# Two chunks of 96 rows, or 128 and 64: the first product of a feed-forward block on TensorE's two halves

## The chip, the core and the metric

The kernel runs on one core of a Trainium2 chip. The metric is the device time of one execution in microseconds (us), and the median of some runs is given. TensorE multiplies matrices (PE in the profile; PEld is its loading of weights), VectorE is DVE, ScalarE is ACT, GpSimd is POOL, and SyncE (SP) issues transfers. The engines run their own streams of instructions and wait for each other by semaphores.

## The reference

A tower of two layers over 16 sequences of 128 tokens with 192 features, all in fp32: token embedding, an attention with running sums, a feed-forward block with a routed attention of its own, a second attention, and a mixture of 8 experts. The change touches the last lines of the feed-forward block:

```python
h = hidden_states + merged
n2 = _ln(h, g2, b2)                       # over 192 features
ffn = jax.nn.gelu(n2 @ W1 + bf1, approximate=False) @ W2 + bf2    # W1: 192 x 768, W2: 768 x 192
return h + ffn
```

## The kernel before

Four sequences make a group (G = 4, 512 tokens), and there are four groups. The stages are written out by hand, one list of calls for each engine. `front` works on group 0 alone. `joint(ta, tb)` runs three times: it lays the first half of the network for group `ta` between the second half for group `tb`, which begins with the feed-forward product. `back` does the second half of the last group alone, with its tokens in two halves of 256 (`hf`), and starts the experts.

The feed-forward product in a joint stage runs so. `n4_T` transposes the normalized tokens `xb` on TensorE into PSUM, two chunks of 96 features for each sequence (C = 2, CW = 96). `n4T_evac` on ScalarE brings them to SBUF in `xT` and applies scale and bias (`g2c`, `b2c`). `ffn_up(tb, j)`, for each of six slices of 128 hidden features (FJ = 6), multiplies 128 x 128 weights `w_up` with all 512 tokens and adds two such products, one for each chunk: the chunks have 96 rows, and rows 96 to 127 of the weights are zero. `ffn_gelu(tb, j)` on ScalarE takes the slice through gelu to `hid` (in the buffer `big`), and `ffn_down(tb, b)` multiplies it by `w_down` once all six gelus are done. The slices lie in the PSUM pairs `PD`, `PC`, `PD`, so slices 4 and 5 wait for gelus 0 and 1.

Between the slices stand two small steps of the other group, and ScalarE has to load another table of functions for each of their steps and back. TensorE: slices 0 to 2, `scores_T`, slices 3 to 5, `scores_back`, `cumulate`, `ffn_down` four times. ScalarE: gelu 0 and 1, `qk_roots` (a square root, L700), `score_exp` (an exponential, L704), gelu 2 to 5 (L791). `scores_back` needs the exponential.

In `back` the same is done by `up_half(tb, j, hf)`, `gelu_half` (L795) and `down_half(tb, b)`: slices 0 and 1 of the first half of the tokens, `n4_T` of the second half, slices 2 to 5, then all six of the second half, each waiting for the gelu that frees its bank, and then the four blocks of the second product.

All matmuls are issued through one helper (L1915), all transposes through another (L1918). The names that a profile shows are those of buffers: `w_up` and `w_down` lie in `arena_e`, PSUM is `qa` (PA and PB) and `qc` (PC and PD).

The experts' first product, `up`, is in both kernels laid out in 128 + 64 rows: six whole matmuls of 128 tokens, then six with 64 rows, by turns from the upper and the lower half of the array, into the two banks of a PSUM pair.

Of the kernel before, what the change touches and what calls it, by code (L numbers as in the profile page):

```python
# [16 lines left out]
ACT = mybir.ActivationFunctionType  # L17
# [3 lines left out]
G = 4  # L21
# [53 lines left out]
def build(nc, a, out):  # L75
    with ExitStack() as ctx:
        def sb(name, shape, dt=F32):
            return ctx.enter_context(nc.sbuf_tensor(name, shape, dt))
# [29 lines left out]
        pos_type = sb("pos_type", [128, D])  # L108
        rows = sb("rows", [128, 5, D])
        gammar, betar, gatewr, wrr, bf2r = (rows[:, k, :] for k in range(5))  # L110
        cols = sb("cols", [CW, 6, C])
        g1c, b1c, g2c, b2c, bqc, bkc = (cols[:, k, :] for k in range(6))
        bf1c = sb("bf1c", [128, FJ])
        sc = sb("sc", [128, 8])
        w_g2b = sb("w_g2b", [KR, D])
# [86 lines left out]
        hb = sb("hb", [128, G, D])  # L202
        xT = sb("xT", [KR, C, G * 128])
        nT = sb("nT", [KR, C, G * 128])
        gT = sb("gT", [KR, G, 128])
        st = sb("st", [128, 3, G, 6])
        mv = sb("mv", [128, 3, 6, G])
# [108 lines left out]
        def part_of(pair, p, b, c, n=128):  # L316
            lo = ((b % 2) * C + c) * n
            return pair[0:p, b // 2, lo:lo + n]

        def half_of(pair, p, hf, n=128):  # L320
            return pair[0:p, hf, 0:2 * C * n].rearrange("p (b c t) -> p b c t", b=2, c=C)

        def chunks(t, hf):
            return t[0:CW, :, hf * 256:hf * 256 + 256].rearrange("p c (b t) -> p b c t", b=2)

        def half(b):
            return b // 2 * 2 + 2
# [4 lines left out]
        def two(hf):  # L332
            return slice(hf * 256, hf * 256 + 256)
# [307 lines left out]
        def _(act):  # L641
# [140 lines left out]
            def n4T_evac(tb, hf):  # L782
                w(tb, "n4T", 2 * hf + 2)
                for c in range(C):
                    i = A(chunks(xT, hf)[:, :, c, :], half_of(PC, CW, hf)[:, :, c, :], ACT.Identity,  # L785
                          bias=b2c[:, c:c + 1], scale=g2c[:, c:c + 1])
                i.then_inc(*done("n2T"))

# [1124 lines left out]
        def _(pe):  # L1913
# [3 lines left out]
            def tr(o, i, k):  # L1917
                return nc.tensor.transpose(o, i, ident[0:k, 0:k])  # L1918
# [4 lines left out]
            def inc(ins, name):  # L1923
                ins.then_inc(s[name], 1)
# [198 lines left out]
            def n4_T(tb, hf):  # L2123
                for b in (2 * hf, 2 * hf + 1):
                    w(tb, "ln4", (18 if tb == NG - 1 else 11) + b + 1)
                    for c in range(C):
                        i = tr(part_of(PC, CW, b, c), xb[:, b, c * CW:(c + 1) * CW], 128)
                    inc(i, "n4T")

            def ffn_up(tb, j):  # L2130
                w(tb, "n2T", 2)
                if j >= 4:
                    w(tb, "gelu", j - 3)
                inc(both((PD, PC, PD)[j // 2][:, j % 2, :], lambda k: w_up[:, k, j * 128:(j + 1) * 128], lambda k: xT[:, k, :]),
                    "up")

            def ffn_down(tb, b):
                w(tb, "gelu", FJ)
# [4 lines left out]
            def up_half(tb, j, hf):  # L2143
                w(tb, "n2T", hf + 1)
                if j == 4:
                    w(tb, "hin", 2 * G)
                if hf:
                    w(tb, "gelu", j + 1)
                inc(both((PD, PA, PB)[j // 2][:, j % 2, two(hf)], lambda k: w_up[:, k, j * 128:(j + 1) * 128],
                         lambda k: xT[:, k, two(hf)]), "up")  # L2150

            def down_half(tb, b):
                w(tb, "gelu", FJ * (b // 2 + 1))
# [491 lines left out]
def _layout(i):  # L2645
# [27 lines left out]
    d["w_l0o"] = by_rows(n["L0_attn_Wo"].T)  # L2673
    d["log_tau"] = n["L0_attn_prior_log_tau"].reshape(H)
    d["mu"] = n["L0_attn_prior_mu"].reshape(1, D)
    d["cols"] = np.stack([col(f + k) for k in ("g1", "b1", "g2", "b2", "bq", "bk")], axis=1)
    d["bf1"] = col(f + "bf1", FJ)
    for k in ("Wq", "Wk"):
        d["f" + k] = by_rows(n[f + k])
    for k, bias in (("Wv", "bv"), ("Wo", "bo"), ("Wm", "bm")):  # L2680
        d["f" + k] = biased(n[f + k], n[f + bias])
    d["W1"] = by_rows(n[f + "W1"])
    d["W2"] = n[f + "W2"].reshape(FJ, 128, D).transpose(1, 0, 2)
    l = "L1_attn_"
    d["M_UV"] = np.stack([n[l + "M_U"].T, n[l + "M_V"]], axis=1)
# [32 lines left out]
```

## Time and profile before

| | |
|---|---|
| median of 3 runs | 846.82 us (845.39 to 847.04) |
| the profiled execution, own time | 845.1 us |
| its span, first to last instruction | 843.2 us |
| TensorE busy | 736.0 us, 87% |
| weight loads (beside the matmuls) | 552.1 us, 65% |
| VectorE busy | 506.9 us, 60% |
| ScalarE busy | 302.5 us, 36% |
| GpSimd busy | 232.9 us, 28% |

A row of the timeline gives the start in us from the span's start, the length in us of all instructions merged in it, the engine, the line, output <- inputs, for a matmul the rows and columns of the array that it uses and then the shape, the number of records (x12), and in brackets how long the engine was idle before it and for what. A matmul's record is longer than its distance to the next, since they are pipelined.

### The profile page before, as it was taken

The numbers are of one execution on the slowest core, as the hardware profiler recorded it, in microseconds if no ns is written. First come the engines' busy times: TensorE is split into PE (matmuls) and PEld (weight loads), VectorE is DVE, ScalarE is ACT, GpSimd is POOL, SyncE is SP. The second block draws the span as 40 slices with busy tenths as digits, with TensorE's granted clock in tenths as the row PEclk, the third lists the DMA queues.
The fourth block names the chain that finished last, engine by engine and source line by source line (L and its number), as shares of the span: only waits on it lengthen the run. The fifth ranks groups of instructions, "written<-read, shape, count | busy, mean of one in ns | idle before, by whom it ended". The sixth has DMA issues, their size and how long they took to land.

```text
span 843.2 us, 16016 instructions
## 1 busy us (share of the span) xinstructions
PE 736.0 (87%) x5742; PEld 552.1 (65%) x5743; DVE 506.9 (60%) x1714; ACT 302.5 (36%) x698; POOL 232.9 (28%) x281
## 2 busy tenths in 40 slices
PE   1798777999889998978999898899989999999992
PEld 0546546565656656655755675677857999999991
DVE  6557668874769797367976546883345643333320
ACT  0023132443443262434326244334233433333330
POOL 5332020443002346101321200132001553444342
PEclk9999899999999999999999999999999999999996
DMA  7960000000000100000010000017601233222220
GB/s 245 413 286 1 1 1 0 20 8 1 2 2 6 52 20 8 1 2 1 25 33 1 1 2 2 1 39 285 184 2 29 49 76 44 43 43 36 38 32 8
DMA packets 29447, 43.11 MB, mean 51 GB/s; under 512 B 5099, under 2 KB 24277, under 8 KB 29382
## 3 DMA queue, kind: packets, MB, share of 16 engines
q1 hardware_dynamic: 19122, 30.87, 10.5%
q0 software_dynamic: 8432, 8.53, 5.8%
q10 hardware_dynamic: 1828, 2.84, 0.9%
q8 instruction: 41, 0.67, 0.3%
q14 instruction: 24, 0.20, 0.1%
HBM read 20.81 MB, written 22.09 MB: 51 GB/s over the span
## 4 chain that ended last, share of the span: by engine, by line
PE 57%; DVE 26%; issue 5%; ACT 4%; POOL 4%; DMA 2%; SPq 1%; DVEq 0%; POOLq 0%; ACTq 0%
PE qa L1915 25%; PE qc L1915 25%; PE qc L1918 4%; PE qa L1918 3%; DVE mx L1493 2%; DVE st L1064 2%; DMA out<-qk_T 1%; DMA mu_row<-in_mu 1%; ACT big L818 1%; POOL arena_w L438 1%; DVE xb L1108 1%; DVE qk_T L1499 1%; POOL rs_a L473 1%; DVE arena_e L1305 1%; DVE ctxT L1448 1%
## 5 line engine op out<-in xcount | busy, mean ns | idle before, releaser
L1915 PE MATMUL qc<-arena_w,big 128*128 x468 | 83.0, 327 | 2.2 <-DVE qk_T L1894 1.4
L1915 PEld LDWEIGHTS qc<-arena_w,big 128*128 128x128 f32 x468 | 75.1, 190 | 3.4 <-issue 3.3
L1915 PE MATMUL qa<-arena_e,nT 128*128 128x192 f32 (+2 forms) x256 | 69.0, 425 | 2.3 <-DVE ga L1375 2.0
L1915 PE MATMUL qa<-arena_b 128*128 128x128 f32 (+2 forms) x688 | 69.9, 281 | 1.0 <-ACT arena_b L775 0.8
L615 POOL DMA_INDIRECT out<-qk_T x39 | 64.4, 1651 | 19.9 <-POOL spare L614 10.7
L1030 ACT ACTIVATE big<-qa,arena_b 128x128 f32<-128x128 f32 x156 | 43.1, 375 | 72.2 <-PE qc L1915 67.3
L1915 PEld LDWEIGHTS qa<-arena_b 128*128 128x128 f32 (+2 forms) x688 | 64.0, 187 | 6.4 <-ACT arena_b L775 1.4
L1915 PEld LDWEIGHTS qa<-arena_e,nT 128*128 128x128 f32 x256 | 46.1, 196 | 24.3 <-issue 14.1
L1894 DVE TENSOR_SCALAR qk_T<-qc,qk_T 128x192 f32<-128x192 f32 x39 | 16.3, 418 | 64.7 <-PE qc L1915 58.3
L473 POOL TENSOR_TENSOR rs_a<-rs_a,minus_half 128x8 f32<-128x8 f32 x4 | 6.6, 1643 | 169.8 <-DVE rs_a L1342 169.8
L1918 PE MATMUL qa<-cst,arena_b 128*128 128x128 f32 (+2 forms) x232 | 33.6, 285 | 9.3 <-DVE arena_e L1305 3.7
L1915 PE MATMUL qc<-w_1q,cst 128*32 128x256 f32 x152 | 40.6, 397 | 0.0
L1493 DVE TENSOR_REDUCE mx<-qc 128x6 f32<-128x768 f32 x28 | 25.5, 954 | 23.9 <-PE qc L1915 23.9
L710 ACT ACTIVATE arena_e<-qa 128x512 f32<-128x512 f32 x42 | 23.4, 595 | 43.0 <-PE qa L1918 42.9
L1918 PEld LDWEIGHTS qa<-cst,arena_b 128*128 128x128 f32 (+2 forms) x232 | 26.0, 143 | 18.9 <-issue 9.6
L518 POOL TENSOR_TENSOR arena_b<-arena_w,ck 128x576 f32<-128x576 f32 x16 | 18.5, 1165 | 67.1 <-DVE cf L1275 54.2
L818 ACT ACTIVATE big<-qc 128x768 f32<-128x768 f32 x28 | 21.2, 808 | 43.7 <-PE qc L1915 43.7
L1915 PE MATMUL qc<-xT,arena_e 128*128 128x512 f32 (+1 forms) x88 | 36.4, 561 | 0.5 <-ACT xT L785 0.4
L1915 PE MATMUL qc<-qk_T 32*128 32x128 f32 (+1 forms) x680 | 28.2, 288 | 8.0 <-DVE qk_T L1499 5.3
L535 POOL DMA_INDIRECT slots<-xk,pos_i x32 | 32.2, 1008 | 10.3 <-issue 9.9
L1915 PEld LDWEIGHTS qc<-qk_T 32*128 32x128 f32 (+1 forms) x680 | 23.0, 186 | 16.7 <-DVE qk_T L1499 10.1
L1030 ACT ACTIVATE big<-qa,big 128x128 f32<-128x128 f32 x78 | 21.5, 373 | 34.0 <-PE qc L1915 34.0
(393 smaller groups left out, 1582.5 us busy)
## 6 DMA issues: line engine op xcount, KB each, us to landing
slots<-xk SPq DMA_DIRECT2D x1, 13192.0 KB, 42.6
arena_e<-in_w SPq DMA_DIRECT2D x8, 579.0 KB, 7.8
arena_w<-in_w SPq DMA_DIRECT2D x8, 576.0 KB, 8.9
qk_T<-slots SPq DMA_DIRECT2D x39, 97.0 KB, 1.9
out<-hb SPq DMA_DIRECT2D x16, 96.0 KB, 1.7
arena_e<-in_w_l SPq DMA_DIRECT2D x1, 804.0 KB
arena_e<-in_W ACTq DMA_DIRECT2D x1, 768.0 KB
out<-qk_T POOLq DMA_INDIRECT x39, 3.6
```

Of the source, the lines that this page charges most:

```text
L473: pool.tensor_tensor(rs_a[:, 1, :, :], rs_a[:, 0, :, :], minus_half.rearrange("p (k b) -> p k b", k=2), ALU.pow).then_inc(s["rstd_a"], 1)
L518: pool.tensor_tensor(qk48[:, b % 2, 1, :, 0:48].rearrange("p h (k d) -> p h k d", k=3), bc(rq[:, b, H:24, :], 2, 3), bc(ck[:, b, :, :], 3, ...
L535: pool.indirect_dma_start(out=slots, out_offset=bass.IndirectOffsetOnAxis(ap=pos_i[:, k, b:b + 1], axis=0), in_=xk[:, k, b, :], in_offset= ...
L615: pool.indirect_dma_start(out=rows_out, out_offset=bass.IndirectOffsetOnAxis(ap=xs[:, u, D + 1:D + 2].bitcast(I32), axis=0), in_=ym[:, u, ...
L710: A(qkTf[:, b % 2, j * 512:(j + 1) * 512], lin(b, wide)[:, j, :], ACT.Copy).then_inc(*done("qk_evac"))
L818: A(eT[:, b % 2, 6 * hf:6 * hf + 6, :].rearrange("p (i j) t -> p i (j t)", i=2), sec(b, wide)[:, 2 * hf:2 * hf + 2, 0:384], ACT.Exp, scale ...
L1030: i = A(hTm[:, u % 2, j, :], PS[u % 2][:, j % 2, j // 2 * 128:j // 2 * 128 + 128], ACT.Gelu, bias=w1s[u % 3][:, F + FJ // 2 * 128 + j:F + ...
L1064: nc.vector.bn_stats(st[:, b, :], src[:, b, :]).then_inc(s[name], 1)
L1493: nc.vector.reduce_max(mx1[:, :, HD].rearrange("p (j i) -> p i j", i=4)[:, 2 * hf:2 * hf + 2, :], sec(b, wide)[:, 2 * hf:2 * hf + 2, 0:384 ...
L1894: TS(ym[:, u, :], PD[:, 1, 0:D], xs[:, u, D:D + 1], None, ALU.mult).then_inc(m_y, 1)
L1915: return nc.tensor.matmul(o, l, r, start=start, stop=stop)
L1918: return nc.tensor.transpose(o, i, ident[0:k, 0:k])
```

## The change

The 192 features are no longer cut in 96 + 96. Chunk 0 holds features 0 to 127 and chunk 1 features 64 to 191, both with 128 rows, so they overlap (`lapped`, done on the host for W1, scale and bias). An even slice takes its main product from chunk 0 (128 rows) and the rest, features 128 to 191, from rows 64 to 127 of chunk 1. An odd slice takes its main product from chunk 1 and the rest, features 0 to 63, from rows 0 to 63 of chunk 0. The two rests of a pair of slices stand behind both main products, use different halves of the array and different PSUM banks. The tokens get a buffer of their own, `wT`, all of whose rows are written; `xT` stays for the later steps, with its constant rows.

```diff
-        cols = sb("cols", [CW, 6, C])
-        g1c, b1c, g2c, b2c, bqc, bkc = (cols[:, k, :] for k in range(6))
+        cols = sb("cols", [128, 6, C])
+        g1c, b1c, bqc, bkc = (cols[0:CW, k, :] for k in (0, 1, 4, 5))
+        g2c, b2c = (cols[:, k, :] for k in (2, 3))
...
+        wT = sb("wT", [128, C, G * 128])
...
+        def wide(t, hf):
+            return t[:, :, hf * 256:hf * 256 + 256].rearrange("p c (b t) -> p b c t", b=2)
...
                 for c in range(C):
-                    i = A(chunks(xT, hf)[:, :, c, :], half_of(PC, CW, hf)[:, :, c, :], ACT.Identity,
+                    i = A(wide(wT, hf)[:, :, c, :], half_of(PC, 128, hf)[:, :, c, :], ACT.Identity,
                           bias=b2c[:, c:c + 1], scale=g2c[:, c:c + 1])
...
-                        i = tr(part_of(PC, CW, b, c), xb[:, b, c * CW:(c + 1) * CW], 128)
+                        i = tr(part_of(PC, 128, b, c), xb[:, b, c * KX:c * KX + 128], 128)
                     inc(i, "n4T")
+
+            rest = (slice(KX, 2 * KX), slice(0, KX))
 
             def ffn_up(tb, j):
                 w(tb, "n2T", 2)
                 if j >= 4:
                     w(tb, "gelu", j - 3)
-                inc(both((PD, PC, PD)[j // 2][:, j % 2, :], lambda k: w_up[:, k, j * 128:(j + 1) * 128], lambda k: xT[:, k, :]),
-                    "up")
+                mm((PD, PC, PD)[j // 2][:, j % 2, :], w_up[:, j % 2, j * 128:(j + 1) * 128], wT[:, j % 2, :], True, False)
+                if j % 2:
+                    for k in (j - 1, j):
+                        inc(mm((PD, PC, PD)[k // 2][:, k % 2, :], w_up[rest[k % 2], 1 - k % 2, k * 128:(k + 1) * 128],
+                               wT[rest[k % 2], 1 - k % 2, :], False, True), "up")
...
-                inc(both((PD, PA, PB)[j // 2][:, j % 2, two(hf)], lambda k: w_up[:, k, j * 128:(j + 1) * 128],
-                         lambda k: xT[:, k, two(hf)]), "up")
+                mm((PD, PA, PB)[j // 2][:, j % 2, two(hf)], w_up[:, j % 2, j * 128:(j + 1) * 128], wT[:, j % 2, two(hf)],
+                   True, False)
+                if j % 2:
+                    for k in (j - 1, j):
+                        inc(mm((PD, PA, PB)[k // 2][:, k % 2, two(hf)], w_up[rest[k % 2], 1 - k % 2, k * 128:(k + 1) * 128],
+                               wT[rest[k % 2], 1 - k % 2, two(hf)], False, True), "up")
...
+    def lapped(m):
+        return np.stack([m[k * KX:k * KX + 128] for k in range(C)], axis=1)
...
-    d["W1"] = by_rows(n[f + "W1"])
+    d["W1"] = lapped(n[f + "W1"])
```

TensorE's order in the first joint stage before, from slice 2 on: one row for each matmul (or run of like ones), its output rows and columns and what it waits for. `es` and `eTs` are `scores_T` and `scores_back`, the last row is the second product.

```order
L1915 MATMUL qc<-xT,arena_e 128x512 [waits n2T]
L1915 MATMUL qc<-xT,arena_e 128x512
L1915 MATMUL qa<-cst,es 48x128 [waits sdot,vug]
L1915 MATMUL qc<-xT,arena_e 128x512 [waits n2T]
L1915 MATMUL qc<-xT,arena_e 128x512
L1915 MATMUL qc<-xT,arena_e 128x512 [waits gelu,n2T]
L1915 MATMUL qc<-xT,arena_e 128x512
L1915 MATMUL qc<-xT,arena_e 128x512 [waits gelu,n2T]
L1915 MATMUL qc<-xT,arena_e 128x512
L1915 MATMUL qa<-cst,eTs 128x48 [waits s_exp]
L1915 MATMUL qa<-es,cst 128x96 [waits smax]
L1915 MATMUL qc<-arena_e,big 128x192 [waits gelu]
```

The same place in the changed kernel, from the first slice on. A row with x2 and no wait behind one with a wait is the pair of rests, whose 64 rows the shape doesn't show, since it is that of the output.

```order
L1920 MATMUL qc<-wT,arena_e 128x512 [waits n2T] x2
L1920 MATMUL qc<-wT,arena_e 128x512 x2
L1920 MATMUL qc<-wT,arena_e 128x512 [waits n2T]
L1920 MATMUL qa<-cst,es 48x128 [waits sdot,vug]
L1920 MATMUL qc<-wT,arena_e 128x512 [waits n2T]
L1920 MATMUL qc<-wT,arena_e 128x512 x2
L1920 MATMUL qc<-wT,arena_e 128x512 [waits gelu,n2T] x2
L1920 MATMUL qc<-wT,arena_e 128x512 x2
L1920 MATMUL qa<-cst,eTs 128x48 [waits s_exp]
L1920 MATMUL qa<-es,cst 128x96 [waits smax]
L1920 MATMUL qc<-arena_e,big 128x192 [waits gelu]
```

The number of matmuls stays at twelve. Ahead of `scores_T` stand five and no longer six, and behind it seven; slice 0 is complete only with the fourth matmul, and slices 4 and 5 are complete together, as the last.

## Rows read from the trace of the kernel before

**Rows 1.** The page: the chain that ended last, by engine.

```profile
PE 57%; DVE 26%; issue 5%; ACT 4%; POOL 4%; DMA 2%; SPq 1%; DVEq 0%; POOLq 0%; ACTq 0%
```

**Rows 2.** Busy time by stretch: length, PE, PEld, DVE, ACT, POOL, clock, DMA.

```profile
164.17:176.23 12.06, 11.76 (x30) 5.15 (x31) 8.83 (x32) 10.63 (x15) 2.84 (x5) 1.00 0.06 15
...
448.89:460.91 12.02, 11.72 (x31) 5.11 (x31) 5.22 (x19) 10.60 (x15) 0.00 (x0) 1.00 0.00 1
577.85:588.75 10.90, 10.90 (x52) 9.60 (x53) 0.02 (x1) 6.86 (x14) 3.33 (x6) 1.00 1.00 392
```

**Rows 3.** Timeline of TensorE's matmuls, first joint stage.

```profile
164.17 5.42 PE L1915 MATMUL qc<-xT,arena_e 128*128 128x512 f32 x12 [0.20 <-ACT xT L785]
169.52 0.42 PE L1915 MATMUL qa<-cst,es 128*48 128x128 f32 x2
169.87 5.42 PE L1915 MATMUL qc<-xT,arena_e 128*128 128x512 f32 x12
175.22 0.42 PE L1915 MATMUL qa<-cst,eTs 48*128 48x48 f32 x2
175.93 0.46 PE L1915 MATMUL qa<-es,cst 128*128 128x96 f32 x2 [0.30 <-DVE es L1257]
176.23 1.01 PE L1915 MATMUL qc<-arena_e,big 128*128 128x192 f32 x5
```

**Rows 4.** Timeline of ScalarE, same stretch.

```profile
166.43 0.69 ACT L791 ACTIVATE big<-qc,bf1c 128x512 f32<-128x512 f32 x1
167.91 0.69 ACT L791 ACTIVATE big<-qc,bf1c 128x512 f32<-128x512 f32 x1 [0.79 <-PE qc L1915]
168.61 1.28 ACT L700 ACT_TABLE_LOAD   x1
...
171.88 1.28 ACT L791 ACT_TABLE_LOAD   x1
173.18 1.84 ACT L791 ACTIVATE big<-qc,bf1c 128x512 f32<-128x512 f32 x3
175.32 0.69 ACT L791 ACTIVATE big<-qc,bf1c 128x512 f32<-128x512 f32 x1 [0.30 <-PE qc L1915]
```

**Rows 5.** Timeline of VectorE behind it.

```profile
175.67 0.21 DVE L1257 COPY es<-qa 128x48 f32<-128x48 f32 x1 [2.22 <-PE qa L1915]
...
184.26 0.62 DVE L1482 TENSOR_TENSOR hb<-hb,qc 128x192 f32<-128x192 f32 x2 [0.97 <-PE qc L1915]
```

**Rows 6.** Timeline of GpSimd behind it.

```profile
186.90 1.05 POOL L477 TENSOR_TENSOR rs_b<-rs_b,minus_half 128x4 f32<-128x4 f32 x1 [1.48 <-DVE rs_b L1077]
```

**Rows 7.** Timeline of TensorE, an expert tile's half matmuls and what follows.

```profile
665.89 0.94 PE L1915 MATMUL qa<-arena_b,big 64*128 64x128 f32 x12
666.76 0.44 PE L1918 MATMUL qc<-cst,qk_T 128*128 128x128 f32 x2
```

**Rows 8.** Timeline of TensorE, the last record ahead of `scores_T`.

```profile
169.00 0.59 PE L1915 MATMUL qc<-xT,arena_e 128*128 128x512 f32 x1
```

**Rows 9.** Timeline of the weight loads behind `scores_T`.

```profile
169.87 0.30 PEld L1915 LDWEIGHTS qc<-xT,arena_e 128*128 128x128 f32 x2 [0.18 <-issue]
170.40 0.19 PEld L1915 LDWEIGHTS qc<-xT,arena_e 128*128 128x128 f32 x1 [0.24 <-issue]
170.83 0.19 PEld L1915 LDWEIGHTS qc<-xT,arena_e 128*128 128x128 f32 x1 [0.24 <-issue]
```

**Rows 10.** Timeline of TensorE, the last stage's first product.

```profile
577.85 1.99 PE L1915 MATMUL qc<-xT,arena_e 128*128 128x256 f32 x8
...
585.30 3.62 PE L1915 MATMUL qa<-xT,arena_e 128*128 128x256 f32 x16
588.75 0.33 PE L1915 MATMUL qc<-arena_e,big 128*128 128x192 f32 x1
```

**Rows 11.** Timeline of ScalarE, the last stage's first gelus.

```profile
582.65 0.84 ACT L795 ACTIVATE big<-qc,bf1c 128x256 f32<-128x256 f32 x2
```

**Rows 12.** Busy time by stretch, PE alone: length, PE, clock, DMA.

```profile
471.68:475.09 3.41, 1.40 (x21) 1.00 0.01 2
475.09:478.50 3.41, 3.38 (x12) 0.50 0.00 0
```

More of the change, by code:

```diff
@@ L2675, in _layout @@
     d["mu"] = n["L0_attn_prior_mu"].reshape(1, D)
-    d["cols"] = np.stack([col(f + k) for k in ("g1", "b1", "g2", "b2", "bq", "bk")], axis=1)
+    def lapped(m):
+        return np.stack([m[k * KX:k * KX + 128] for k in range(C)], axis=1)
+    cols = np.zeros((128, 6, C), np.float32)
+    for k, name in enumerate(("g1", "b1", "g2", "b2", "bq", "bk")):
+        if name in ("g2", "b2"):
+            cols[:, k, :] = lapped(n[f + name].reshape(D))
+        else:
+            cols[0:CW, k, :] = col(f + name)
+    d["cols"] = cols
     d["bf1"] = col(f + "bf1", FJ)
```

## Prediction

> **What bounds the kernel now.** I read the page's chain of waits first: TensorE carries 57% of it and VectorE 26% [rows 1]. Then I asked for the four stretches that the change touches: the feed-forward's first product in the three joint stages, from its first matmul to that of the second product (12.06 us in the first, 12.02 in the third; the second is a copy of the first), and in the last stage (10.90 us) [rows 2]. In all of them TensorE is busy nearly throughout and its clock is granted in full, so at first sight each matmul that goes is time won. But ScalarE is busy for 10.6 of the 12 us too, and the reader is to see what with [rows 4]: gelu 0 and 1, then a table load, the square root, a table load, the exponential of the scores, a third table load (171.88), and only then gelu 2 to 5. Gelu 0 starts at 166.43, when its table has come. Gelu 1 (167.91) waits for TensorE, gelus 2 to 4 (173.18, three in 1.84 us) wait for nothing but ScalarE's own queue, and gelu 5 (175.32) waits for TensorE again, for 0.30 us. The second product needs all six. It starts at 176.23 [rows 3], 0.22 us after gelu 5 has ended (175.32 + 0.69 = 176.01). So both engines arrive at this point almost together, and a faster TensorE alone gains only what ScalarE lets through.
>
> **What follows the second product.** VectorE adds its result at 184.26, after 0.97 us idle for TensorE [rows 5], and the root on GpSimd waits 1.48 us for VectorE's variances [rows 6]; GpSimd's gathers aren't what is late. So what the second product starts earlier, the rest of a joint stage should start earlier. In the last stage TensorE runs on without a gap to the second product at 588.75 [rows 10].
>
> **Prices of a matmul.** One fp32 matmul leaves two records. At 512 columns a record starts every 0.43 us and lasts 0.59 (12 records in 5.42 us [rows 3]; weight loads at 170.40 and 170.83 [rows 9]). At 256 columns it is 0.216 us (16 records from 585.30 to 588.75 [rows 10]). A matmul with 64 rows at 512 or 256 columns stands nowhere in the trace; the nearest is the expert stage, where 12 records of 64 rows and 128 columns, the two halves in turn, take 0.87 us from 665.89 to 666.76 [rows 7]. One after another at the full array's pace (0.43 by 128/512, 0.108 us a record) they would take 1.29. Two by two they are six steps, 0.65 us, and 0.22 remains. I read that remainder as the two costs of a change between whole and half array. First, the next matmul starts 0.09 us late: the last 512-column record starts at 169.00 and the differently shaped one behind it at 169.52 [rows 8, 3], 0.52 and not 0.43. Second, the weights of the second record aren't loaded ahead: the first load after a change starts at 169.87 and the third, which goes with the second record's start, at 170.40, 0.53 later and not 0.43 [rows 9], so 0.10. 0.09 + 0.10 is 0.19, near the 0.22.
>
> **The change, part by part.** Before, six `ffn_up` of two whole matmuls are 24 records. Now each pair of them has two whole matmuls (four records) and two half ones (four records in two steps). A pair costs 4 x 0.43 + 0.10 (weights after the return) + 0.09 + 0.43 + 0.10 + 0.43 + 0.09 = 2.96 us against 8 x 0.43 = 3.44. The third pair is followed by `scores_back`, a 48-row matmul for which the array changed before too, so it is worth 0.19 more. TensorE's own gain is 3 x 0.48 + 0.19 = 1.6 us in a joint stage.
>
> What of it arrives. The first pair: records at 164.17, 164.70, 165.13, 165.56, the halves at 166.08 and 166.61, which end at 167.20. Before, the eighth record started at 167.28 and ended at 167.87, and gelu 1 started 0.04 later. Now gelu 0 and gelu 1 become ready together: gelu 0 at 167.24 (0.8 later than before), gelu 1 0.58 behind it at 167.82, which is 0.09 earlier than before. The table loads and the exponential behind gelu 1 move by these 0.09 and no more (VectorE's inputs to them are ready: `scores_T` now starts at 168.2, not 169.52). So gelu 2 starts at 173.09 and gelu 5 at 173.09 + 3 x 0.58 = 174.83, no longer waiting for TensorE, whose last pair ends at 173.7. It ends at 175.52, 0.49 earlier than 176.01. The second product then hangs on ScalarE. I give it 0.06 for the release (an estimate; a gelu follows TensorE by 0.04) and 0.10 for weights that aren't ahead, in place of the 0.22 of before: 0.49 + 0.06, about **0.55 us in a joint stage, 1.65 in three**. The lower bound of this term is nothing (if the first halves ran 0.5 us later than I say, gelu 5 would end when it does now); the upper one is TensorE's 1.6.
>
> The last stage: a pair costs 4 x 0.216 + 0.10 + 0.09 + 0.216 + 0.10 + 0.216 + 0.09 = 1.68 us against 1.73, six pairs, **0.3 us**. The price of the changes eats nearly all of what the overlap gives at this width. Its first gelus are ready from 582.65 [rows 11], before the second half's matmuls need their banks (583.3 by these prices), so no wait is added. Gelu 10 and 11 now come together at the end, but two blocks of the second product (24 records of 0.163 us) lie ahead of the one that needs them.
>
> Nothing is priced for the rest. The four transposes of a half load 128 columns and not 96, but stream 128 as before. ScalarE's two evacuations have 128 partitions at the same 256 elements. W1 and the columns are loaded as the kernel begins and first used around 160. That the tokens have a buffer of their own removes no wait, since the order of TensorE and ScalarE already kept the old one free.
>
> The sum is 1.65 + 0.3 = 1.95 us. The profiled execution took 845.1 us (its span 843.2, 1.9 around it) and would take 843.1; the median of the runs shown is 1.7 above it, so the forecast for it is 846.8 - 1.95 = **844.9 us**.
>
> **A rule of the skill against the rows.** The rows show 0.19 us at a change between whole and half array [rows 8, 9]. The Trainium skill, TensorE: Matmul & The Clock Gate, Measured speedup vs the span model, gives tiles in different rows the time of one matmul and 4 ns for each further tile, and nothing for going there and back; its page TensorEngine Tiling (Array Packing), Key Properties, says that changing the tiling mode drains TensorE, without a price. The trace agrees with the second. By the first alone a pair would be 6 x 0.43 = 2.58 us (1.30 at 256 columns), which is the second rival below.
>
> **The rivals.** *TensorE's whole gain arrives*: 3 x 1.6 + 0.3 = 5.1 us, 841.7. For it speaks that VectorE idles 2.22 us until `scores_back` [rows 5] and so starts its coefficients 1.6 us earlier. Against it, those aren't what the rest waits for, and ScalarE's queue is. 8%. *The changes of the array cost nothing*: the halves end 0.19 earlier, gelu 1 starts at 167.63 and gelu 5 ends 0.69 earlier, 0.75 a stage with the release; six pairs of the last stage give 0.43 each. 2.25 + 2.6 = 4.8 us, 842.0. The rows speak against it. 4%. *It is lost behind*: the joint stages' later waits, on VectorE above all, take the 0.55 back and only the last stage's 0.3 is left, 846.5. 18%; the idle times of rows 5 and 6 speak against it, but only for the 10 us after the product. *Slower, the halves don't overlap at these widths*: each half record then takes its own step. Gelu 1 starts 0.2 later and the last pair ends 0.9 later than before; three stages lose 0.9 each. A pair of the last stage costs 2.01 us, 0.28 more than now, six 1.7. 4.4 us, 851.2. It decides once the two halves take some 0.6 us a pair more than the 1.05 I give them. The 0.87 us for 12 records speaks against it. 5%. *Slower, the clock*: once, after a stretch with TensorE busy for 1.40 of 3.41 us, 3.41 us were granted at 0.50, 1.2 GHz [rows 12]. TensorE now idles some 0.9 us more ahead of the second product; if the clock fell there in each stage, up to 1.7 us each were lost: 844.9 + 5.1 = 850.0. 5%.
>
> **How the numbers follow.** The forecast's own case holds 60%, between 843.8 and 846.0. A measurement tells about 0.2%, 1.7 us, from no change, and the forecast is only just beyond it: of the 60 I put 36 beyond (faster) and 24 within. Faster: 36 + 8 + 4 = 48%. Same: 24 + 18 = 42%. Slower: 10%. The range goes from 842.0, which takes in the free changes and leaves most of the first rival out, to 847.3, the lost gain with the runs' own scatter; the slower cases are left out.
>
> **What the changed kernel's profile would show.** In a joint stage: records of 64 rows and 512 columns in twos, some 0.97 us from the first to the last one's next start, and 0.52 us ahead of them; gelu 1 at 3.65 us after the first matmul (3.74 before); gelus 2 to 5 without a gap; the second product 11.5 us after the first matmul and not 12.06, with TensorE idle before it; `scores_back` 1.6 us earlier. In the last stage 10.6 us and not 10.90. The prediction is wrong if the halves stand one behind the other, if gelu 5 still waits for TensorE, or if the three joint stages shorten by other than some 0.55 us each.

## The result, and the profile after

The changed kernel took 851.7 us in the median of 14 runs (847.79 to 854.04), the kernel before 847.25 us in the median of 14 (845.17 to 851.30, and one execution of 911.68). The ratio is 1.0053, with a 95% interval of 1.0036 to 1.0071: slower by half a per cent, and outside the predicted 842.0 to 847.3 us. The profiled execution took 851.78 us, its span is 850.0, and its mean granted clock is 0.961, where that of before had 0.974.

The page of the changed kernel, busy time by engine, to be held against the table of before:

```profile
PE 741.6 (87%) x5742; PEld 551.9 (65%) x5743; DVE 507.1 (60%) x1714; ACT 301.9 (36%) x698; POOL 232.8 (27%) x281
```

TensorE is busy for 5.6 us more (736.0 before), though the product that was changed is shorter. The first product itself, from its first matmul to the second product's, answers to [rows 2]; columns as there:

```profile
165.12:176.52 11.40, 10.16 (x31) 3.69 (x31) 9.83 (x33) 10.40 (x15) 2.82 (x5) 1.00 0.06 16
...
453.43:464.80 11.37, 10.12 (x31) 3.66 (x31) 6.28 (x20) 10.38 (x15) 0.00 (x0) 1.00 0.01 1
584.82:595.37 10.55, 10.55 (x52) 6.26 (x53) 0.00 (x1) 6.29 (x13) 3.31 (x6) 1.00 0.99 392
```

11.40 us against 12.06 and 10.55 against 10.90, with the clock in full. TensorE's timeline of the first joint stage, against [rows 3], and its groups of matmuls with their shapes apart:

```profile
165.12 4.10 PE L1920 MATMUL qc<-wT,arena_e 128*128 128x512 f32 x10 [0.22 <-ACT wT L790]
169.14 0.42 PE L1920 MATMUL qa<-cst,es 128*48 128x128 f32 x2
169.49 5.16 PE L1920 MATMUL qc<-wT,arena_e 128*128 128x512 f32 x14
174.49 0.32 PE L1920 MATMUL qa<-cst,eTs 48*128 48x48 f32 x2
175.11 0.46 PE L1920 MATMUL qa<-es,cst 128*128 128x96 f32 x2 [0.30 <-DVE es L1262]
176.51 1.73 PE L1920 MATMUL qc<-arena_e,big 128*128 128x192 f32 x9 [0.94 <-ACT big L796]
```

```profile
L1920 PE MATMUL qc<-wT,arena_e 128*128 128x512 f32 x12 | 6.2, 627 | 0.2 <-ACT wT L790 0.2
L1920 PE MATMUL qc<-wT,arena_e 64*128 64x512 f32 x12 | 3.4, 641 | 0.0
```

And ScalarE in the same stretch, against [rows 4]:

```profile
168.19 1.27 ACT L796 ACTIVATE big<-qc,bf1c 128x512 f32<-128x512 f32 x2 [0.83 <-PE qc L1920]
169.47 1.28 ACT L705 ACT_TABLE_LOAD   x1
...
172.74 1.28 ACT L796 ACT_TABLE_LOAD   x1
174.04 2.42 ACT L796 ACTIVATE big<-qc,bf1c 128x512 f32<-128x512 f32 x4
```

`scores_back` is at 9.37 us after the first matmul (11.05 before), gelus 2 to 5 follow one another without a gap, and the second product waits for ScalarE. So the place that was changed does what was forecast. Where did the time go? The same view over the whole joint stages, of before and then of the changed kernel:

```profile
164.17:306.29 142.12, 128.15 (x1028) 88.03 (x1029) 104.91 (x374) 57.45 (x113) 39.16 (x50) 1.00 0.05 13
306.29:448.89 142.60, 129.66 (x1029) 88.87 (x1029) 105.19 (x373) 57.58 (x113) 37.24 (x48) 0.99 0.04 12
448.89:577.85 128.96, 117.60 (x975) 80.30 (x975) 86.83 (x310) 51.69 (x100) 21.66 (x27) 0.97 0.05 17
```

```profile
165.12:309.75 144.63, 131.06 (x1029) 90.17 (x1029) 105.38 (x375) 57.36 (x113) 39.22 (x50) 0.96 0.04 13
309.75:453.43 143.68, 129.80 (x1029) 88.36 (x1029) 104.46 (x373) 57.34 (x113) 37.27 (x48) 0.98 0.04 12
453.43:584.82 131.39, 119.25 (x976) 81.12 (x975) 87.15 (x310) 51.61 (x100) 21.78 (x27) 0.95 0.05 17
```

As many matmuls, but a lower clock (the column behind POOL's): 0.96 and not 1.00 in the first stage, and the three stages take 6.0 us more. In the first, every milestone stands 0.6 us earlier than before up to the router's gate (96.67 us after the stage's start, 97.26 before); from there to `gates_T`, 2.8 us later than before (110.05, 107.25). What lies between is `gate`, with 8 streamed columns a matmul (`w_gate` in its records), and `select`, with 20 (`pw`). TensorE alone, just ahead of this place and in it, of the changed kernel:

```profile
260.98:264.40 3.42, 3.42 (x33) 1.00 0.02 5
264.40:274.64 10.24, 10.24 (x46) 0.50 0.00 1
```

and of before, at the same distance from the stage's first matmul (the second row starts 99.28 us after it there and 99.30 here):

```profile
260.05:263.47 3.42, 3.42 (x31) 1.00 0.00 0
263.47:273.71 10.24, 9.18 (x71) 1.00 0.03 10
```

In the one 10.24 us are granted at 0.50, 1.2 GHz, and only 46 of 71 records are done in them, in the other the clock stays at 2.4 GHz. The busy time ahead is the same, but the work is not, since the changed kernel comes to it 0.6 us earlier. TensorE's timeline of the two stretches ahead, of the changed kernel and then of before:

```profile
260.81 1.14 PE L1920 MATMUL qa<-arena_e,nT 128*128 128x192 f32 x6
261.78 1.85 PE L1920 MATMUL qc<-w_gate,xT 128*128 128x8 f32 x16
263.49 1.13 PE L1920 MATMUL qa<-pw,xn 128*96 128x20 f32 x11
```

```profile
259.80 0.49 PE L1918 MATMUL qc<-cst,xk 128*96 128x128 f32 x3
260.13 1.47 PE L1915 MATMUL qa<-arena_e,nT 128*128 128x192 f32 x8
261.43 1.85 PE L1915 MATMUL qc<-w_gate,xT 128*128 128x8 f32 x16
263.13 0.49 PE L1915 MATMUL qa<-pw,xn 128*96 128x20 f32 x4
```

Both have the 16 records of `gate`; the changed kernel has 11 of `select` with them and before only 4, with more records of 128 and 192 columns in their place. Traces of the runs below, on other chips where before takes 847 us, agree: third_after and fourth_after have 13 and 12 records of `select` there and lose the clock, at_par_2, whose stage stands as before's, has 4 and keeps it. And in the 3.41 us just ahead of each of the 22 falls at this place, in nine traces (before, the changed kernel's three, at_par, at_par_2, half_lead, later_still and gate_par), 11 to 16 records of `select` start and 9 to 16 of `gate`.

Over the three joint stages 30.7 us are at half clock, 10.2 before. None of these stretches lies in the changed product. In these two traces they begin at two places of a stage: 26 us after its start, around the waits of `kq` and `x5_T` (the first weak place below), and 99 to 101 us after it, at `gate` and `select` (the second). At before's clock the stages would be some 1.7 us shorter than before (0.61, 0.57 and 0.56 us, measured below), and they are 6.0 longer: the 20.5 us more at half clock cost 7.7 us. The Trainium skill, TensorE: Matmul & The Clock Gate, Terms, has the penalty as about the throttled time times the share that isn't granted. With half of it here that is an estimate of 10.2 us; the stages show less. That TensorE isn't what is waited for in part of the time at half clock would explain it; no run here shows it.

### The profile page after: what moved, and what is told of

The parts are those of the page before. It is cut to its first block, busy times and chain, and to the rows that moved or that the text cites. A ratio compares the mean times of both kernels' runs of the same rounds, so it can differ in the third digit from the quotient of the medians.

```text
span 850.0 us, 16016 instructions
## 1 busy us (share of the span) xinstructions
PE 741.6 (87%) x5742; PEld 551.9 (65%) x5743; DVE 507.1 (60%) x1714; ACT 301.9 (36%) x698; POOL 232.8 (27%) x281
## 4 chain that ended last, share of the span: by engine, by line
PE 60%; DVE 22%; issue 6%; ACT 4%; POOL 3%; DMA 2%; SPq 1%; DVEq 0%; POOLq 0%; ACTq 0%
PE qa L1920 27%; PE qc L1920 26%; PE qc L1923 4%; PE qa L1923 3%; DVE mx L1498 2%; DVE st L1069 2%; DMA out<-qk_T 1%; ACT big L823 1%; DVE xb L1113 1%; DMA mu_row<-in_mu 1%; POOL arena_w L443 1%; DVE arena_e L1310 1%; DVE qk_T L1504 1%; POOL rs_a L478 1%; DVE ctxT L1453 1%
## 5 line engine op out<-in xcount | busy, mean ns | idle before, releaser
L1923 PE MATMUL qa<-cst,arena_b 128*128 128x128 f32 (+2 forms) x232 | 34.1, 288 | 9.5 <-DVE arena_e L1310 4.0
L1920 PE MATMUL qc<-arena_e,big 128*128 128x192 f32 x192 | 32.3, 328 | 2.8 <-ACT big L796 2.8
```

Of the source, the lines that this page charges most:

```text
L1920: return nc.tensor.matmul(o, l, r, start=start, stop=stop)
```

## The experiments

A **hold** is a matmul on constants whose result nobody reads, as the kernel has them already; one is two records of 256 columns, 0.43 us. In my first expectations I took it for half of that, so the fills there are twice as long as they say.

**First chip: is the idle time ahead of the second product what lowers the clock?** The changed kernel's TensorE idles for 0.94 us there, as its timeline above shows. Three kernels with holds ahead of the second product, and the changed kernel again.

```diff
                 cumulate(ta)
+                hold(QA[:, 3, :], 5)        # fill5; 8 in fill8; 3 in before_late, in the kernel before
                 ffn_down(tb, 0)
```

> The changed kernel once more, beside before on one chip. What the two profiles show so far: the second product starts 11.40 us after the first matmul in joint stage 1 (12.06 before), so the change does there what was forecast, and TensorE's clock was granted at half for some 20 us more. Theory 1 (the lost time is clock): about 851 to 852 us, some 4 us above before, the mean clock some 0.01 lower, and the joint stages' first products again 0.6 us shorter. Theory 2 (the first comparison was scatter between chips): within 1 us of before or below it, at equal mean clock.

> The changed kernel with five filler matmuls (128 x 32, 256 columns, 1.08 us) where TensorE idles 1.1 us ahead of the second product, into a free bank; the product should start when it does now. Theory 1a (the clock falls later because of this new idle time): back to 845 to 846 us. Theory 1b (the clock falls because of where the free-running stretches of the clock meet weak stretches of the kernel, and the shift of 0.6 us a stage alone moves these): unchanged, 851 to 852. Theory 1c (the half-array matmuls themselves count for less): unchanged too.

> The changed kernel with eight fillers (1.73 us) there, so that the second product starts as late as before the change (12.06 us after the first matmul). Everything behind it then stands where it stood before. Theory 1b (place, not activity): the time of before, 847 (up to 0.3 us below it for the last stage). Theory 1c (activity of the halves): still about 851. Theory 1a: 846 to 847 too.

> The kernel before with three fillers (0.65 us) ahead of the second product in each joint stage: everything behind comes 0.65 us later, 1.95 us in all. With no effect of the clock: 849.2. Theory 1b: it deviates from before + 1.95 us by more than 1.5 us, in either direction, at a mean clock that differs by some 0.004 or more. Theories 1a and 1c: 849.2 at the clock of before.

Before took 868.33 us on this chip (29 runs). The changed kernel: 864.69 us, 0.9957 [0.9943, 0.9972], *faster*, with a mean clock of 0.954 where before has 0.955. That is what theory 2 had said, but the chip is 20 us slower for both kernels, so it doesn't answer the comparison. fill5: 870.71 us, 1.0030 [1.0018, 1.0041], its second product at 12.66 us. fill8: 869.78 us, 1.0016 [1.0006, 1.0026], at 13.96. before_late: 868.39 us, 1.0000 [0.9988, 1.0013], at 13.57. Filling the idle time doesn't help on this chip; fill8 moved the second product 1.9 us past its place in before, so it is no test of theory 1b. And in before_late the second product comes 1.5 us later in each of three stages, 4.5 us in all, for nothing in the total (its mean clock is 0.959, before's 0.955), so here a move of this size was swallowed or outweighed.

**Second chip: both kernels once more, and both with the weak places filled.**

```diff
+                hold(QA[:, 3, :], 1)
                 kq(ta, 0)
+                hold(QA[:, 3, :], 2)
                 x5_T(tb, 0)
+                hold(QA[:, 3, :], 2)
                 x5_T(tb, 1)
+                hold(QA[:, 3, :], 1)
...
+                hold(QC[:, 3, :], 2)
                 gate(tb)
+                hold(QC[:, 3, :], 3)
                 select(ta)
...
                 probs_T(ta, 1)
+                hold(QC[:, 3, :], 4)
                 context(ta, 0)
```

> The kernel before once more, so that its trace and that of the changed kernel come from one chip, and so that the ratio of two identical kernels is known. Every theory expects 1.000, within 0.2%. Its three joint stages should have the second product 12.06, 12.06 and 12.03 us after the first matmul. If the ratio is off by more than 0.2%, the 1.0053 of the comparison can be scatter alone.

> The changed kernel once more, beside the kernel before on this chip. My theory (the change gives 0.55 to 0.66 us in each joint stage and 0.35 in the last, and the sign of the total is made by how long the clock is granted at half in weak stretches elsewhere): second product at 11.40 us, last stage 10.55, and a total within 0.6% of before on either side, with the difference of the two traces following their sums of stretches at half clock, about half of that sum's difference. Rival, that the half-array matmuls themselves are slower or pull the clock down: slower than before by 0.5% on this chip as in the comparison, with a stretch at half clock in or right behind the first product in at least one joint stage.

> The kernel before with matmuls on constants (a hold is two records of 256 columns, 0.43 us, its result unused) in the places of a joint stage where TensorE does little: 1 ahead of kq(0), 2 ahead of each x5_T, 1 behind them, 2 ahead of gate, 3 ahead of select, 4 ahead of context. They are 15 holds, 6.5 us of TensorE in each stage, some of it in its idle time. My theory: the stretches at half clock in the joint stages (some 20 us in all in before's trace, 40 to 50 on the other chip) mostly go. Each 3.41 us at half costs up to 1.7 us, so the kernel ends between 5 us slower (holds paid, nothing regained) and 10 us faster.

> The changed kernel with the same holds in the same places. To be read against the one above it: my theory expects that with the stretches at half clock gone or alike in both, it ends 3 x 0.6 + 0.35, about 2 us, earlier than the kernel before with holds (0.2%). Rival, the change costs something of its own: it ends 3 to 5 us later than that one (the 0.5% of the comparison).

Before: 868.46 us (30 runs). Its copy: 0.9995 [0.9979, 1.0011]. The changed kernel: 865.84 us, 0.9964 [0.9946, 0.9982], faster again. With holds, before takes 867.54 us (mean clock 0.975) and the changed kernel 865.59 (0.974): 1.95 us between them, which is 3 x 0.6 + 0.35 = 2.15 within the scatter.

**Why are these chips 20 us slower?** The trace of copy_before agrees with that of before to 0.04 us up to `probs_T` of the first joint stage (115.88 and 115.84 us after its start). Then, in TensorE's and ScalarE's timelines of copy_before:

```profile
280.88 1.00 PE L1918 MATMUL qa<-cst,arena_b 114*128 114x114 f32 x8
285.06 1.84 PE L1915 MATMUL qa<-arena_b 128*96 128x114 f32 x8 [3.18 <-ACT arena_b L775]
...
284.45 0.99 ACT L775 ACTIVATE arena_b<-qa 128x456 f32<-128x456 f32 x2 [8.01 <-remote]
```

and of before:

```profile
280.01 1.00 PE L1918 MATMUL qa<-cst,arena_b 114*128 114x114 f32 x8
281.26 1.02 PE L1915 MATMUL qa<-arena_b 128*96 128x114 f32 x8 [0.25 <-ACT arena_b L775]
...
280.66 0.99 ACT L775 ACTIVATE arena_b<-qa 128x456 f32<-128x456 f32 x2 [5.07 <-PE qa L1918]
```

ScalarE starts its copy 3.6 us after TensorE's transposes began and not 0.65 us; VectorE stands still for 1.5 us in the same stretch, and both are released by something that the profile calls remote. This comes in every joint stage of every trace of these two chips, and in none of the others. Behind it the clock falls too, at a third place that the other chips don't have. What it is, none of my runs tells. But it shows why the clock's loss can arrive there in part only: in the first joint stage of copy_after 10.24 us are at half clock behind the gate, as in the comparison, and `gates_T` is 2.78 us later than in copy_before; `context` behind the stall is 0.81 us later, and the stage ends 1.14 us *earlier* (145.99 and 147.13); copy_before has its fall behind the stall instead.

**Third chip, of the comparison's kind.** In lean_after the fills are thinner: 1 and 2 ahead of `x5_T`, 1 ahead of `gate`, 1 ahead of `select`, 2 ahead of `context`.

> The changed kernel a fourth time. The kernel before took 847 us where it came out slower by 0.5%, and 868 us on the two chips where it came out faster by 0.4%; on these both VectorE and ScalarE stood still for some 3 us ahead of the context product in each joint stage (probs_T to context 4.2 us and not 1.2). If the kernel before takes 868 us here too, I expect 0.9945 to 0.998 again. If it takes 847 us, the stall is absent, and what the clock takes back arrives in full: then 0.998 to 1.006, and slower only with more stretches at half clock than before has. Rival, a cost of the half-array matmuls: slower wherever before is fast.

> The kernel before with the 15 holds in each joint stage again (0.998 of before on the last chip). If before takes 868 us here: 0.997 to 0.999. If it takes 847 us, there is no stall that hides the four holds ahead of context, and I expect 1.000 to 1.008.

> The changed kernel with the same holds. It was 1.95 us ahead of the kernel before with holds on the last chip (865.59 to 867.54), as 3 x 0.6 + 0.35 says. I expect 1 to 3 us again, whatever the chip, since its clock hardly falls in the joint stages. Rival: on a chip where the stall is absent the change costs, 3 us or more the other way.

> The changed kernel with fewer holds: 1 ahead of x5_T(0), 2 ahead of x5_T(1), 1 ahead of gate, 1 ahead of select, 2 ahead of context, 3.0 us of TensorE in each joint stage instead of 6.5, of which the two ahead of context and most of those ahead of x5_T lie in idle time. If the holds ahead of gate and select were what the fuller set paid most for, it keeps most of the clock and ends 1 to 4 us ahead of the changed kernel without holds; if the clock falls at the gate again, it ends level with it.

Before: 846.65 us (23 runs). The changed kernel: 850.74 us, 1.0040 [1.0019, 1.0061]. Before with holds: 853.21, 1.0075 [1.0062, 1.0089]; the changed kernel with holds: 851.57, 1.0064 [1.0051, 1.0077], 1.64 us ahead of it (5 and 6 executions). In both traces no stretch of a joint stage is below full clock, so they are the clean comparison. The three joint stages, of warm_before_2 and then of warm_after_2 (whose first products take 12.06 and 11.39 us):

```profile
164.36:309.69 145.33, 134.99 (x1059) 91.08 (x1059) 105.15 (x374) 57.53 (x113) 39.14 (x50) 1.00 0.05 13
309.69:455.10 145.41, 135.09 (x1059) 91.11 (x1059) 105.32 (x373) 57.65 (x113) 37.19 (x48) 1.00 0.04 12
455.10:587.86 132.76, 122.39 (x1005) 81.20 (x1004) 86.84 (x310) 51.77 (x100) 21.64 (x27) 1.00 0.05 16
```

```profile
163.92:308.64 144.72, 133.47 (x1058) 89.76 (x1058) 105.02 (x375) 57.27 (x113) 39.12 (x50) 1.00 0.05 13
308.64:453.48 144.84, 133.57 (x1059) 89.80 (x1059) 105.22 (x373) 57.38 (x113) 37.15 (x48) 1.00 0.04 12
453.48:585.68 132.20, 120.89 (x1006) 79.94 (x1004) 86.78 (x310) 51.50 (x100) 21.64 (x27) 1.00 0.05 17
```

The stages are 0.61, 0.57 and 0.56 us shorter: this is the change at full clock, to each stage's end. The rival of a cost in the half-array matmuls falls with this pair. The thinner fills didn't pay: 850.44 us, 1.0041 [1.0021, 1.0062], a miss of my hope for 1 to 4 us. The holds cost what the clock gave back (mean clock 0.973).

**Fourth chip: the lead taken away, all else of the change kept.** In at_par the second product starts at 12.07 us, as before.

```diff
+                hold(QA[:, 3, :], 3)        # at_par and half_lead
+                short(QA[:, 3, :], 160)     # at_par alone: one matmul of 160 columns
                 ffn_down(tb, 0)
...
+                hold(QC[:, 3, :], 1)        # gate_par alone
                 gate(tb)
```

> The changed kernel with 3 holds and one matmul of 160 columns on constants ahead of the second product, so that it starts 12.06 us after the first matmul, as in the kernel before; all that follows in a joint stage then stands where it stood before the change, and only the last stage keeps its 0.35 us. My theory (the 0.6 us lead moves the weak stretch at the gate to where the clock falls in it): on a chip where before takes 847 us the ratio goes from 1.004 back to 0.999 to 1.001, the joint stages take 142.1, 142.6 and 129.0 us as in before, and no 10 us at half clock stands behind the gate of the first. Rival, the half-array matmuls or the wider evacuation cost something or lower the clock by themselves: it stays at 1.003 or more. On a chip where before takes 868 us: 0.999 to 1.001, and not 0.996.

> The changed kernel with one hold ahead of gate, which took 0.65 us there in the kernel with the fewer holds: the lead of 0.6 us lasts to x6_T and is spent just ahead of the gate, so gate and select stand at 97.3 and 99.0 us as in before. My theory: where before takes 847 us, 0.998 to 1.002, with the first joint stage at 142.1 to 142.8. If it stays at 1.004 with the clock falling behind the gate as in the changed kernel, the place of the gate isn't what decides, and the lead acts earlier in the stage.

> The changed kernel with 3 holds ahead of the second product, which then starts at 11.8 us, between 11.40 and 12.06. If the clock's falls depend on the place of the weak stretch by tenths of a us, it ends between the changed kernel and at_par where before takes 847 us, 1.000 to 1.004, its single runs more spread than those of either; if it equals the changed kernel (1.004) or at_par (1.000) to 0.1%, the border lies on one side of it.

Before: 846.49 us (23 runs). at_par: 847.40 us, 1.0006 [0.9988, 1.0024], mean clock 0.973 (before 0.971). half_lead, its second product at 11.80 us: 849.30 us, 1.0020 [0.9996, 1.0043], clock 0.967. gate_par: 851.65 us, 1.0065 [1.0040, 1.0091], clock 0.967. The times of the first two are as my theory says, the trace of at_par is not: its joint stages take 144.10, 144.29 and 128.99 us, where I expected 142.1, 142.6 and 129.0, and have six stretches of 3.41 us at half clock where before has three. The third is a miss: with `gate` at 97.32 us as in before, the clock didn't fall in the first stage (142.29 us); but in the third it fell at both weak places, for 6.83 us each, and in the second where the second product starts. TensorE alone, ahead of that fall and in it:

```profile
315.35:318.76 3.41, 2.17 (x10) 1.00 0.00 0
318.76:322.17 3.41, 3.41 (x12) 0.50 0.00 0
```

So the gate's place isn't all of it; the falls at the first weak place count as well, and the lead is still there when it comes. (The traced execution took 849.0 us, the shortest of six.)

The holds of at_par take away two things, the lead and TensorE's 0.94 us of idle time. The idle time is filled in half_lead too (neither trace has a gap there), and half_lead keeps 0.27 us of the lead. Its mean clock is 0.967 and at_par's 0.973, over 12 executions each, a difference of four times its standard error. So the place counts with the idle time gone in both; a kernel with the idle time and without the lead was not run.

**Fifth chip: with and without the lead side by side, and a move the other way.** later_still is fill5 again.

> The changed kernel with its lead spent ahead of the second product, beside the changed kernel itself on one chip, which the last runs did not have. Where before takes 847 us: 0.999 to 1.002, and 2 to 5 us below the changed kernel. Where before takes 868 us: 0.998 to 1.001 and 1 to 4 us above it, since there the lead is worth what the trace of a stage says.

> The changed kernel: 1.003 to 1.006 where before takes 847 us, with a mean granted clock 0.005 to 0.01 below before's; 0.994 to 0.998 where it takes 868 us, at before's clock.

> The changed kernel with 5 holds ahead of the second product, which starts at 12.66 us, 0.6 us later than in before and not earlier (it was 1.003 of before where before takes 868 us). If only the place of what follows decides the clock, this can go either way where before takes 847 us: 0.6 us later in each stage is 1.8 us to pay, so 1.001 to 1.003 with before's clock, 1.006 or more if the clock falls here too. If leading is what costs (an earlier second product, whatever the place), the clock is before's and it ends at 1.001 to 1.003.

Before: 846.78 us (28 runs). Without the lead: 846.69 us, 1.0000 [0.9984, 1.0016], mean clock 0.972. With it: 851.89 us, 1.0047 [1.0025, 1.0069], clock 0.962. The two lie 5.2 us apart, and the slower one has 1.6 us less of work for TensorE in each joint stage. 0.6 us later than before: 850.00 us, 1.0039 [1.0021, 1.0056], clock 0.970. That is 3.2 us, where 1.8 are paid in three stages and 0.35 won in the last, with the clock hardly lower than before's. It lies between my two expectations and decides little: moving later costs its own length and some more. The stretches at half clock in the joint stages, of fourth_after and then of at_par_2:

```profile
264.36:274.60 10.24, 10.24 (x45) 7.77 (x45) 7.76 (x48) 3.03 (x9) 1.27 (x2) 0.50 0.00 1
336.04:339.45 3.41, 3.21 (x7) 1.92 (x8) 3.29 (x7) 0.89 (x2) 1.67 (x4) 0.50 0.00 0
411.13:414.54 3.41, 3.41 (x15) 1.94 (x14) 3.20 (x30) 0.88 (x3) 0.00 (x0) 0.50 0.01 2
479.40:482.81 3.41, 3.21 (x11) 2.00 (x11) 2.53 (x4) 1.78 (x3) 0.00 (x0) 0.50 0.03 5
554.49:564.73 10.24, 10.24 (x44) 7.27 (x42) 8.37 (x47) 3.36 (x15) 2.77 (x4) 0.50 0.06 19
```

```profile
409.12:412.53 3.41, 3.41 (x13) 1.89 (x12) 3.10 (x29) 0.90 (x4) 0.00 (x0) 0.50 0.01 2
477.39:480.80 3.41, 3.39 (x12) 2.40 (x13) 2.92 (x5) 1.78 (x3) 0.00 (x0) 0.50 0.00 0
552.48:555.89 3.41, 3.41 (x13) 1.72 (x11) 3.23 (x27) 0.94 (x4) 0.00 (x0) 0.50 0.01 2
```

The changed kernel's falls are the five of the comparison's trace at the same distances from the stages' starts to 0.1 us, and those of third_after to 0.15; at_par_2 has before's three, to 0.1 us. The changed kernel has its pattern wherever before takes 847 us, in three traces of three, and the kernel with the lead taken away has before's in one trace of two (the other has falls at both places in all three stages, 3.41 us each, and 845.4 us of span all the same).

All executions of the third, fourth and fifth chips say it without the traces. Of 74 executions of before, 61 have a mean clock of 0.969 or more; of 38 of the changed kernel (the comparison's 14 with them) one has, and that one took 844.59 us. A straight line through both sets, with time falling by 5.4 us for each 0.01 of clock, leaves the changed kernel 0.6 us *faster* at equal clock (standard error 0.25). The 0.008 that its clock lies lower (0.9626 and 0.9706) are 4.3 us. The 0.6 us are short of the 1.95 us that the change gives at full clock: the means lie 3.7 us apart, 5.7 with the gain that didn't arrive, and the mean clock accounts for 4.3 of them; the other 1.3 stay open.

## Why the prediction was wrong

**The prices were right.** Step by step, forecast and then trace: the last whole record to the first half 0.52 us, 0.52; the pair of half records and the way back 1.05 us, 1.06 (the records start at 167.03, 167.56 and 168.09); gelu 1 3.65 us after the first matmul, 3.66 (the two gelus take 1.27 us from 168.19, the second of them the last 0.69); gelus 2 to 5 without a gap, so; `scores_back` 1.6 us earlier, 1.68; the second product 11.5 us after the first matmul, 11.40; the last stage 10.6 us, 10.55. The way from the third pair to `scores_back` costs nothing extra (174.06 to 174.49, 0.43 us), as the sum had it. The term "0.55 us in a joint stage" measured 0.66 at the second product and 0.6 at the stage's end.

**What failed is the step behind them**, in the prediction's words: "what the second product starts earlier, the rest of a joint stage should start earlier". It took the clock of all that follows to stay what it was. Up to the first weak place it holds in every trace of the changed kernel. From there the 0.6 us decide which work lies ahead of the times at which the clock falls, and so in which stretches it does: the joint stages did not shorten by 0.55 us each but grew by 2.5, 1.1 and 2.4. What that costs, 7.7 us in the profiled execution and at least 4.3 in the mean, is two to four times the 1.95 us that there were to gain. The runs that show it: the change is worth 1.6 and 1.95 us between kernels whose joint stages are filled; and with the lead taken away (and the idle time filled) the ratio goes from 1.0047 back to 1.0000 on one chip, with the half-array matmuls still in it.

**The rivals.** "Slower, the clock" had the right engine, and nearly the time (850.0), at the wrong place: it expected the fall ahead of the second product, where the idle time was new. The one fall at that place stands in the second stage of gate_par; filling it (fill5, fill8) gave nothing on a chip where before takes 868 us; where it takes 847 us, later_still, the kernel of fill5, has nearly before's clock and is 3.2 us slower than before. I had read one stretch at half clock [rows 12] as a risk that idle time brings, and not asked where in a stage the kernel's other stretches stand and whether they would still be there after a shift. "The halves don't overlap" is refuted by the records (641 ns mean, two at a time). "It is lost behind" is right in that the gain was gone at the stages' ends, but it had waits on VectorE as the reason. The two faster rivals fell with ScalarE's queue.

**What stays open.** The busy time ahead of the fall doesn't tell the two kernels apart, the number of narrow matmuls in it does, in all the traces named above. But why the falls come at the times at which they come, and why some last 10.24 us and others 3.41, no run tells. My reading, argued and not shown: the decision comes at times that the kernel doesn't set, and the program's place against them is carried over from one execution to the next, since joint stage 1 begins 33.69 to 33.85 us after the last stretch at half clock of the front has ended, in before, in the comparison's trace, in third_after and in fourth_after alike (and in half_lead, gate_par and later_still too, each with a pattern of its own). That would be why executions repeat the pattern and the median doesn't average it out. at_par_2 has another distance (26.84 us) and before's pattern all the same; at_par, at 33.98 us, has neither pattern. gate_par and later_still show that I can't say from a shift's size alone which pattern it brings. Open too is the stall ahead of `context` on the two slower chips, and with it which kind of chip the kernel should be tuned for: the change is faster by 0.4% on those two and slower by 0.4 to 0.5% on the others. No version here beats both kernels on both kinds; on the faster kind at_par equals before and only one execution of the changed kernel in 38 had the clock that most of before's have (844.59 us).

## What to carry to other kernels

Before you sum up a gain of a few tenths of a us per stage, list the stretches at half clock of the whole trace with their distance from the stage's start, and treat every one behind the edit as able to move, vanish or double; here that term was two to four times the edit's own. Look at which matmuls stand ahead of such a stretch, not only at how busy the engine is. Test an edit at full clock, with both kernels' weak stretches filled, to learn what it is worth, and with its lead taken away to learn what the clock makes of it. And a sign that rests on one chip isn't yet a sign: repeat it on a second before explaining it.

## What the runs showed of the hardware

- The clock fell while the records show TensorE without a gap: 3.42 us busy of 3.42, with 16 records of 8 columns and 11 of 20 among them, and then 10.24 us at 0.50. With the 16, only 4 of 20 columns and more of 128 and 192 in the same busy 3.42 us, it stayed at full. The Trainium skill, TensorE: Matmul & The Clock Gate, HAM oscillation — how this bites in real kernels, tells of the fall as what waits bring, when TensorE stands idle for long; ahead of this fall the trace has no such wait.
- A change between 128-row and 64-row matmuls costs 0.09 us to the first one and 0.10 more ahead of the second: 0.52 and 0.53 us between records that are 0.43 apart otherwise, five times in each joint stage: ahead of each pair of halves and behind the first two. From the third pair to a matmul with 48 rows it is 0.43.
- Two chips ran the same kernel in 868 us, three others and that of the first comparison in 847. The three joint stages take 18.9 us of it (432.58 and 413.68 us), some 10 by a stall of 2.9 to 3.9 us in each, much of the rest with the clock at half (34.1 us of them in copy_before, 10.2 in before).
- Two matmuls of 64 rows, in different halves of the array and with results in different banks, ran side by side: their four records start at 167.03, 167.04, 167.56 and 167.57. The gelus that read the neighbouring banks keep their pace (two in 1.27 us, four in 2.42; three in 1.84 before).
